# Keeping the last chunk's first-layer results in SBUF for the perceptron, and writing the output tile by tile

## What is computed

```
agg = einsum('nm,bmd->bnd', A_hat, h)          # h = relu(layernorm(x))
z   = agg.reshape(-1, d) @ W1.T                # 128 -> 256
h   = relu(batchnorm(z + b1, g1, be1))         # statistics over all 8*2048 rows
out = batchnorm(h @ W2.T + b2, g2, be2)        # statistics over all rows again
x   = x + out.reshape(8, 2048, 128)
```

## Time and profile before

| | us |
|---|---|
| median of 3 runs (lowest to highest) | 3039.32 (3038.06 to 3040.39) |
| the profiled execution, its own time | 3033.48 |
| its span in the profile | 3031.7 |
| granted TensorE clock, mean over the span | 0.968 |

### The profile page before, as it was taken

The page is one execution under the profiler, slowest core; times in us unless marked ns, Lnnn a source line. Parts: engine busy times, 40 slices in busy tenths (PEclk is TensorE's granted clock), DMA queues, the critical chain, the costliest instruction groups (busy, mean ns, idle before and its releaser), DMA issues. The chain is left out here.

```text
span 3031.7 us, 38525 instructions
## 1 busy us (share of the span) xinstructions
PE 2749.6 (91%) x14565; PEld 2319.6 (77%) x14565; DVE 1659.9 (55%) x3195; ACT 1323.7 (44%) x2150; POOL 171.7 (6%) x98
## 2 busy tenths in 40 slices
PE   6799998899999969999999996998989868999987
PEld 6678887899999958888877875777777757778743
DVE  8766765577777643213322124888787863331246
ACT  2665454566666532112211113666767663221235
POOL 2000102000001000000000000001010000000000
PEclk9999997999999979999999998999999989999999
DMA  8544543322223153223322113011212135231258
GB/s 347 175 152 164 179 163 142 101 69 85 70 70 98 43 179 110 66 64 136 111 73 65 55 66 139 15 42 28 84 28 56 28 83 193 94 95 48 87 197 304
DMA packets 240837, 326.18 MB, mean 108 GB/s; under 512 B 13680, under 2 KB 155024, under 8 KB 235920
## 3 DMA queue, kind: packets, MB, share of 16 engines
q1 hardware_dynamic: 237200, 311.25, 31.7%
q10 hardware_dynamic: 3456, 12.58, 1.0%
HBM read 227.17 MB, written 96.62 MB: 107 GB/s over the span
## 5 line engine op out<-in xcount | busy, mean ns | idle before, releaser
L986 PE MATMUL l_acc<-l_a_hi,l_g_hi 128*128 128x512 f32 x1536 | 602.3, 392 | 38.0 <-DVE l_g_lo L917 28.7
L986 PE MATMUL l_acc<-l_a_lo,l_g_hi 128*128 128x512 f32 x1536 | 599.2, 390 | 0.0
L986 PE MATMUL l_acc<-l_a_hi,l_g_lo 128*128 128x512 f32 x1536 | 598.8, 390 | 0.0
L909 DVE TENSOR_TENSOR l_a_lo<-l_raw,l_a_hi 128x512 fp32r<-128x512 f32 x192 | 132.8, 691 | 752.9 <-ACT l_a_hi L859 752.9
L1442 PE MATMUL n_acc<-n_hb,n_p 128*128 128x129 f32 x4096 | 472.6, 276 | 24.7 <-DVE n_p L1358 19.5
L859 ACT ACTIVATE l_a_hi<-l_raw 128x512 fp32r<-128x512 f32 x192 | 121.1, 631 | 845.6 <-PE l_acc L986 818.8
L1442 PEld LDWEIGHTS n_acc<-n_hb,n_p 128*128 128x128 f32 x4096 | 464.5, 192 | 28.8 <-issue 15.1
L986 PEld LDWEIGHTS l_acc<-l_a_hi,l_g_hi 128*128 128x128 f32 x1536 | 289.3, 188 | 99.8 <-DVE l_g_lo L917 28.9
L1358 DVE SCALAR_TENSOR_TENSOR n_p<-n_e,n_cols,c_mT 128x2048 f32<-128x2048 f32 x128 | 296.8, 2346 | 89.3 <-ACT n_e L1319 71.0
L2053 ACT ACTIVATE r_gate<-r_ps,r_bias 128x512 f32<-128x512 f32 (+2 forms) x504 | 297.1, 639 | 110.6 <-PE r_ps L2214 77.4
L986 PEld LDWEIGHTS l_acc<-l_a_lo,l_g_hi 128*128 128x128 f32 x1536 | 289.3, 188 | 61.1 <-issue 1.4
(11 more groups left out here) (261 smaller groups left out, 3782.7 us busy)
## 6 DMA issues: line engine op xcount, KB each, us to landing
l_raw<-in_adjT_dram SPq DMA_DIRECT2D x256, 256.0 KB, 2.8
l_raw<-in_rows_dram SPq DMA_DIRECT2D x64, 256.0 KB, 3.0
l_hraw<-h SPq DMA_DIRECT2D x32, 512.0 KB, 3.4
z<-l_res SPq DMA_DIRECT2D x64, 256.0 KB, 2.7
m_z<-z SPq DMA_DIRECT2D x16, 1024.0 KB, 5.0
l_xt<-in_x_dram SPq DMA_DIRECT2D x30, 512.0 KB, 3.4
d_xt<-in_x_dram SPq DMA_DIRECT2D x16, 512.0 KB, 18.2
n_hb<-h SPq DMA_DIRECT2D x8, 1024.0 KB, 5.8
```

The source lines that it names most:

```text
L909: dve.tensor_tensor(a_lo[:, gp % RING], raw[:, gp % RING], a_hi[:, gp % RING].bitcast(F32), ALU.subtract).then_inc(a_low, 1)
L986: last = pe.matmul(acc[:, b], lhs[:, s, b * D:(b + 1) * D], rhs[:, gp % RING], start=(s == 0 and lhs is g_hi and rhs is a_hi), stop=(s == ...
```

## The change

The stage `spread` gets its `g_lo` handed in, allocated just before by `network` and released at once, so that a second tensor `lasting` (16 x 1024 floats a partition, the same 64 KB) lies on the same SBUF addresses. For the last chunk ACT copies the 16 units not into the ring `res` but into the upper half of `lasting` (at that time `g_lo` has been used for the last time), without the two waits for a free ring slot; DVE takes the statistics from there; SP doesn't store that chunk to `z1`, and its wait at the end is for the stores of chunks 0 to 2.

In `perceptron` the four tiles of the last chunk (KEPT) are done first, with ACT reading them from `lasting`; the other twelve (COMING) follow from `z` as before. `x_all` is now a view of `lasting`: tile t of `x3` goes to the t-th 4 KB of it, so the upper half can be filled only when the kept tiles have been used. SP's order of loads becomes: z tiles 0 and 1, x tiles 0 to 3, then for t from 2 to 11 z tile t (once ACT has used z tile t - 2) and x tile t + 2, then x tiles 14 and 15. `o2` and its statistics keep their places by tile number. The output tensor has the layout (tile, partition, batch, feature), so a tile's store has 4 KB in one run per partition; the host turns it round.

```diff
@@ spread
+        stored = len(chunks) - 1 if deep else len(chunks)
+
+        def result(ch, r):
+            u = units_at[ch] + r
+            if ch < stored:
+                return res[:, u % OUT]
+            k, b = r // 8, r % 8
+            return lasting[:, HALF + b // 2 * 2 + k, b % 2 * CW:(b % 2 + 1) * CW]
...
-            store(len(chunks) - 1)
-            last = units_at[-1]
+            if stored == len(chunks):
+                store(len(chunks) - 1)
+            last = units_at[stored]
...
-                        if u >= OUT:
+                        if u >= OUT and ch < stored:
                             act.wait_ge(res_out[u % OUT], 16 * (u // OUT))
                             act.wait_ge(po_read, u - OUT + 1)
-                        act.activation(res[:, u % OUT], acc[:, r % 8], ACT.Copy).then_inc(res_ready, 1)
+                        act.activation(result(ch, r), acc[:, r % 8], ACT.Copy).then_inc(res_ready, 1)
...
@@ perceptron
-        x_all = prog.sb(ctx, "m_x_all", [P, T, B, D])
+
+        KEPT = CH
+        COMING = T - KEPT
+        x_all = lasting[:, :, :].rearrange("p t (b f) -> p t b f", f=D)
+        kept = lasting[:, HALF:T, :].rearrange("p (q k) w -> p q k w", k=2)
...
-            run_slots(sp, load, T, 2, 2)
-            for t in range(HALF, T):
-                sp.dma_start(x_all[:, t], io["x3"][t]).then_inc(x_in[1], 16)
+            def load_x(t):
+                sp.dma_start(x_all[:, t], io["x3"][t]).then_inc(x_in[t // HALF], 16)
+
             def load(t):
+                if t >= 2:
+                    sp.wait_ge(h_ready, 2 * KEPT + t * 2 - 2)
+                sp.dma_start(z[:, t % 2], io["z1"][t]).then_inc(z_in[t % 2], 16)
+            load(0)
+            load(1)
+            for t in range(4):
+                load_x(t)
+            for t in range(2, COMING):
+                load(t)
+                load_x(t + 2)
+            for t in range(COMING + 2, T):
+                load_x(t)
 
             def store(t):
                 sp.wait_ge(x_done, t.n + 1)
-                sp.dma_start(out_tiles[t.n], x_all[:, t.n]).then_inc(x_out, 16)
+                sp.dma_start(out[t.n], x_all[:, t.n]).then_inc(x_out, 16)
...
+            for q in range(KEPT):
+                for k in range(2):
+                    if k == 0 and q >= 2:
+                        act.wait_ge(o_summed, q * 2 - 2)
+                    act.activation(hid[:, q % 2, k], kept[:, q, k], ACT.Relu, bias=aff[:, k, 1:2],
+                                   scale=aff[:, k, 0:1]).then_inc(h_ready, 1)
+
             def hidden(t):
...
-            run_slots(act, hidden, T, 2, 2)
+            run_slots(act, hidden, COMING, 2, 2)
...
@@ network
-        spread(prog, io, keep, "l3", [dict(kind="L3", h=io["h3"], w=w1)])
-        perceptron(prog, io, keep, dict(w2=w2, vec=vec), out)
+
+        with ExitStack() as place:
+            g_low_part = prog.sb(place, "l3_g_lo", [P, T, W], F32R)
+        lasting = prog.sb(ctx, "lasting", [P, T, W])
+        spread(prog, io, keep, "l3", [dict(kind="L3", h=io["h3"], w=w1)], g_low_part, lasting)
+        perceptron(prog, io, keep, dict(w2=w2, vec=vec), out, lasting)
...
@@ kernel
-    out = nc.dram_tensor("out_0_dram", (B, N, D), F32, kind="ExternalOutput").ap()
+    out = nc.dram_tensor("out_0_dram", (T, P, B, D), F32, kind="ExternalOutput").ap()
```

More of the change, by code:

```diff
@@ L719, in _, with spread @@
             dot(CH - 1)
-def spread(prog, io, keep, name, jobs):
+def spread(prog, io, keep, name, jobs, g_low_part=None, lasting=None):
     nc = prog.nc
@@ L737, in spread @@
         g_hi = prog.sb(ctx, n_("g_hi"), [P, T, W], F32R)
-        g_lo = prog.sb(ctx, n_("g_lo"), [P, T, W], F32R)
+        g_lo = prog.sb(ctx, n_("g_lo"), [P, T, W], F32R) if g_low_part is None else g_low_part
         raw = prog.sb(ctx, n_("raw"), [P, RING, CW])
@@ L941, in finish @@
                         dve.wait_ge(res_ready, u + 1)
-                        dve.bn_stats(keep["bn1"][:, r // 8, c * 8 + r % 8, :], res[:, u % OUT]).then_inc(po_read, 1)
+                        dve.bn_stats(keep["bn1"][:, r // 8, c * 8 + r % 8, :], result(ch, r)).then_inc(po_read, 1)
                         continue
@@ L2232, in _, with perceptron @@
             pairs(pe, slot, 1)
-def perceptron(prog, io, keep, weights, out):
+def perceptron(prog, io, keep, weights, out, lasting):
     nc = prog.nc
@@ L2257, in perceptron @@
         y_ready, turned, x_done = (sem(s) for s in ("y_ready", "turned", "x_done"))
-        out_tiles = out.rearrange("b (t p) f -> t p b f", p=P)
         ident = keep["ident"]
@@ L2306, in _ @@
             act.wait_ge(aff_own, 12)
+            for q in range(KEPT):
[4 more added lines that the diff above has]
+                                   scale=aff[:, k, 0:1]).then_inc(h_ready, 1)
             def hidden(t):
                 for k in range(2):
-                    if k == 0 and t.within(2, T):
-                        act.wait_ge(o_summed, t.n * 2 - 2)
+                    if k == 0:
+                        act.wait_ge(o_summed, t.n * 2 + 2 * KEPT - 2)
                     act.wait_ge(z_in[t.par], t.pair * 16 + 16)
@@ L2335, in _, with collect @@
                 affine(dve, k, keep["bn1"][:, k].rearrange("p c s -> p (c s)"), 3 * k)
-            def collect(t):
+            def collect(at, n):
                 for c in range(2):
[L2339 to L2343, removed]
+                    dve.wait_ge(o_summed, n * 2 + c + 1)
+                    dve.tensor_scalar(o2[:, at, c * 512:(c + 1) * 512], po[:, c], 1.0, None, ALU.mult)
+                    dve.bn_stats(bn2[:, at * 2 + c], po[:, c]).then_inc(o_read, 1)
+            for q in range(KEPT):
+                collect(COMING + q, q)
+            run_slots(dve, lambda t: collect(t.n, t.n + KEPT), COMING, 2, 2)
             dve.wait_ge(o_read, 2 * T)
@@ L2355, in _, with multiply @@
             pe.wait_ge(w_in, 16)
-            def multiply(t):
+            def multiply(n, par, first):
                 for c in range(2):
                     for k in range(2):
[L2360 to L2363, removed]
+                        pe.wait_ge(h_ready, n * 2 + k + 1)
+                        if k == 0 and not first:
+                            pe.wait_ge(o_read, n * 2 + c - 1)
+                        last = pe.matmul(po[:, c], w2[:, k], hid[:, par, k, c * 512:(c + 1) * 512],
                                          start=(k == 0), stop=(k == 1))
                     last.then_inc(o_summed, 1)
-            run_slots(pe, multiply, T, 2, 2)
+            for q in range(KEPT):
+                multiply(q, q % 2, q == 0)
+            run_slots(pe, lambda t: multiply(t.n + KEPT, t.par, False), COMING, 2, 2)
             def final(t):
@@ L2453 @@
             for k, v in lay.items()}
-    out = nc.dram_tensor("out_0_dram", (B, N, D), F32, kind="ExternalOutput").ap()
+    out = nc.dram_tensor("out_0_dram", (T, P, B, D), F32, kind="ExternalOutput").ap()
     network(nc, out=out, **args)
     r = _run(nc, [{f"in_{k}_dram": v for k, v in lay.items()}], core_ids=[0])
-    return r.results[0]["out_0_dram"][:, column]
+    return r.results[0]["out_0_dram"].transpose(2, 0, 1, 3).reshape(B, N, D)[:, column]
```

## The result

| | before | changed |
|---|---|---|
| median of 9 runs each (lowest to highest), us | 3038.06 (3035.2 to 3040.59) | 3030.1 (3025.11 to 3031.08) |
| the profiled execution, us | 3033.48 | 3027.22 |
| its span, us | 3031.7 | 3025.4 |

The ratio of the changed kernel to the one before is 0.9975, 95% interval 0.9966 to 0.9983: some 7.6 us faster, about half of the 15.1 forecast. The time of 3030.1 lies near the upper end of the stated range, 3020.5 to 3031.0. The profiled executions differ by 6.3 us of span, and the stages say where.

A forecast was written before the change was run, and what follows sets the result against it. PE was busiest at 91% of the span, but the touched last 130 us had three stretches, each with its own limit. The terms -1.9 - 4.7 - 8.5 = -15.1 took 3039.3 to 3024.2 us, range 3020.5 to 3031.0.

The forecast's parts named there:

- Start of the perceptron, -1.9: Before the hidden loop: without the last chunk's stores and 2.3 us wait, first DMA at 2918.4 instead of 2920.3, -1.9 us.
- Unchanged slow first tile: First hidden tile: PE's pause gets 1.9 us shorter but stays long, so the half-clock tile was costed as unchanged.
- Hidden loop, -4.7: DVE's first to last read: 60.0 us falls to 55.3, tiles 0 to 5 at 3.49, then 3.77 each.
- the prediction's own sign: Hidden loop: the prediction is wrong if first reads from tile 6 on lie over 4.3 us apart.
- the two limits: Hidden loop from tile 6: queue at 417 GB/s, 3.77 us a tile; ring of two, (4.8 + 2.4) / 2 = 3.6.
- The far bound of that step: Hidden loop: a landing of 7.1 us on every tile, 4.75 a tile, 10.0 late, loop 64.1, +4.1 us.
- the rival of `x3` in front of `z`: Hidden loop: doubled `x3` delays `z`; 3028.9 at half the bad bound, 3033.0 at full; chance 0.15.
- Output, -8.5: Final drain: 4 KB pieces at 404 GB/s, last store lands 3.4 us after the last add, not 11.9; -8.5 us.
- That the output doesn't drain faster: Rival at the drain: 512 B already at line rate or runs not joined; only -6.6 remains, 3032.7; chance 0.08.
- That each `z` lands as late as 11.1 us: Rival in the hidden loop: 6.75 us a tile, loop 82.1, whole +11.7, 3051.0; chance 0.03.
- half of that rival: Hidden loop with half the way to the bad bound: 0 instead of -4.7, sum -10.4, 3028.9 us.

The follow-up runs named there:

- ring of three: The changed kernel with three `z` tiles in the ring instead of two, loads still alternating z, x; 3019.95 us, ratio to before 0.9936.
- the kernel before with a ring of four: The kernel before with the new output layout and four `z` tiles in the ring, nothing kept on chip; 3022.99 us, ratio to before 0.9943.
- the throwaway transposes: Against the ring of four: PE does 48 transposes of the identity before the hidden loop and 28 behind it; 3015.92 us, ratio to before 0.9920.
- the first experiment: Changed kernel with SP's load order altered: x tiles 0 to 7 after z 0 and 1, then z 2 to 11, then x 8 to 15; 3020.63 us.
- the ring of four: The changed kernel with four `z` tiles in the ring instead of two, loads still alternating z, x; 3020.43 us, ratio to before 0.9942.

## Why the prediction was right or wrong, step by step

**Start of the perceptron, -1.9: right.** SP's first DMA came at 2918.22, 0.29 us after DVE's last statistics ended (2917.24 + 0.69 = 2917.93). I had put 0.6 there. It is 0.3 in every kernel that keeps the tiles and 2.5 in every other one, so the store and its wait were what held the stage. DVE then waited 1.86 us for `vec` where it was 4.10; up to the first read the gain is 2.0.

**Unchanged slow first tile: a small miss.** I costed the first tile as before because the pause stays long. But starting 2 us earlier gave PE 2.4 us more at half clock (5.74 against 3.35), and the second read came 1.1 us later behind the first. The ring of three shows that this is what mostly came, not what must come. The +0.5 between last read and last add is not the change's: that stretch took 27.6 to 27.8 us in six of the profiled executions and 28.1 to 28.3 in five, among these the kernel before with a ring of four. What differs is again the time at half clock behind the second pause, 2.78 us in the profile before and 4.62 in the one after; the throwaway transposes took it away (26.7).

**Hidden loop, -4.7: wrong, +3.9.** The tiles 0 to 5 ran as the step said. Wrong were the 4.8 us for a landing (6.9 in the median) and the 417 GB/s of the queue (342). By the prediction's own sign, first reads over 4.3 us apart from tile 6 on, the step failed: they were 4.50 apart. The 417 (not quite the best rate in the rows, which have 433 over 2.3 us) was taken from a stretch in which eight `x3` tiles stood in the queue, all issued ahead; in a ring of two nothing is issued ahead. The step weighed the two limits one by one, the queue's rate (3.77 a tile) and the way through the ring (3.6), and took the larger. In fact they act together: a `z` can't be issued until ACT is done with the tile two before, by then an `x3` stands ahead of it, and its landing grows. Why it grows by more than the `x3`'s 1.3 us stays open. With the measured landing, the step's own formula gives (6.9 + 2.4) / 2 = 4.65 us a tile; 4.50 were measured. The pieces add up: 54.1 at PE's pace, 1.1 for the clock, and 9 x (4.50 - 3.49) = 9.1 make 64.3 against 64.0. The far bound of that step (a landing of 7.1 on every tile, +4.1) was the case that came, and the rival of `x3` in front of `z` had it at its full price, -6.3 in all, as the profile shows. That the two meet to the tenth is chance: the bound has 10.0 us of landings, the loop lost 9.1 to them and 1.1 to the clock. I had set its landings aside because later ones in the loop before were at 4.8. There, though, two `z` followed each `x3`, and 7.1 wasn't one landing alone. The tile view of `z` in the kernel before, from 2932 to 2950, has four loads:

```profile
DMA to landing us min/median/max: 5.8/6.4/7.1
```

The warning stood in the trace, and the step read only the one below 5 us that came later.

**Output, -8.5: right.** 404 GB/s in 4 KB pieces against 285 in 512 B and 282 with the layout undone, 3.5 us from the last add to the end of the span against 12.3, and the layout undone alone brings 11.7 back. The Trainium skill (page "DMA: Bandwidth & Descriptors", section Specifications) has 512 B as enough for line rate; these stores differ, and the measurement decides.

**The rivals.** That the output doesn't drain faster fell. That each `z` lands as late as 11.1 us didn't come. What came is the doubled `x3` in front of `z`, with a chance of 0.15 against the forecast's 0.72. So the measured time lies in the stated range for the wrong reason: the start and the output came as forecast, the loop didn't, and the range holds the time because it had been stretched to 3031.0 to take in half of that rival. What was left out of the sum altogether is that SP's DMA queue stands still for 11 us, from 2931 to 2942, and then can't make up for it: half of `x3` could have been loaded there, as the first experiment does (with other tiles moved behind the loop).

## What to carry to other kernels

A loop fed through a ring of two is paced by (landing + use) / 2, and the landing in that formula is the one with the new neighbours in the queue, not the one in the old trace: price a transfer that is put between two loads of a ring by what it does to the landing, or give the ring one tile more, which took the question away here. Look for stretches in which the DMA queue is idle before moving loads into a stretch in which it is the bound. A store in long contiguous pieces can be worth more than reuse on chip: here 8.6 us alone, where the kept tiles gave 2 us and took back 4 through the order of loads that came with them.

## What the runs showed of the hardware that I had not expected

With 1 MB and 512 KB loads in turn, the rate of one DMA queue depended on how far ahead they were issued: 342 GB/s at a lead of some 4.6 us, 418 at 8.1, 406 at 11.6. Without the 512 KB loads in between, the 1 MB loads landed after 4.8 us at the short lead too. TensorE's granted clock didn't come back earlier for an earlier start in the changed kernel: 0.50 for 3.35 us of work before the change, for 5.74 after it. In the ring of three it was 0.50 for 2.93 us. Throwaway transposes in the pauses kept it at 1.00 and saved 3.5 us against the ring of four.
